# Routing stage of a decoder kernel: earlier gate loads, clearing on GpSimd, tables' arithmetic behind the counts, four context products ahead of them

## The reference, cut to what matters

```python
logits = x @ gate_w.T                      # 2048 tokens, 16 experts
expert, weight = argmax(logits), max(softmax(logits))
place = running count of earlier tokens with the same expert
keep  = place < 160                        # 160 = int(1.25 * 2048 / 16)
y[token] = weight * (relu(x @ w1[expert]) @ w2[expert]) if keep else 0
```

## Time and profile before

| | |
|---|---|
| median of 3 runs | 2365.23 us |
| lowest and highest | 2355.63 and 2367.0 us |
| the profiled execution, its own time | 2356.12 us |
| its span on the core | 2354.3 us |
| busy: PE, DVE, ACT, POOL | 2101.9, 1593.6, 1002.9, 886.1 us |
| the block `moe_route` in the trace | from 721.2 to 772.8 us |

### The profile page before, as it was taken

The page is one execution under the profiler, slowest core; times in us unless marked ns, Lnnn a source line. Parts: engine busy times, 40 slices in busy tenths (PEclk is TensorE's granted clock), DMA queues, the critical chain, the costliest instruction groups (busy, mean ns, idle before and its releaser), DMA issues. The chain is left out here.

```text
span 2354.3 us, 33922 instructions
## 1 busy us (share of the span) xinstructions
PE 2101.9 (89%) x12230; PEld 1455.0 (62%) x12230; DVE 1593.6 (68%) x4159; ACT 1002.9 (43%) x2133; POOL 886.1 (38%) x545
## 2 busy tenths in 40 slices
PE   8688888899996899698996888999898899999996
PEld 3255555554663799466483444448556788888886
DVE  6799999833657112556128996706687988888886
ACT  2498988623866231365425775241102221222110
POOL 0298888401642895333103665414211111110110
PEclk9799999999998999899997999999999999999998
DMA  3131111000005567300101000020300000000001
GB/s 103 47 94 50 50 50 47 17 12 1 1 1 194 188 227 231 117 2 2 61 1 43 1 1 23 21 81 1 143 1 3 1 1 1 1 1 1 1 1 37
DMA packets 63514, 109.35 MB, mean 46 GB/s; under 512 B 12530, under 2 KB 44146, under 8 KB 61620
## 3 DMA queue, kind: packets, MB, share of 16 engines
q1 hardware_dynamic: 61812, 102.99, 13.4%
q0 software_dynamic: 1536, 4.20, 0.5%
HBM read 94.19 MB, written 12.98 MB: 46 GB/s over the span
## 5 line engine op out<-in xcount | busy, mean ns | idle before, releaser
L781 POOL TENSOR_TENSOR XT<-mamba_DU,scan_BS 128x1024 f32<-128x1024 f32 x128 | 299.2, 2361 | 141.9 <-DMA scan_BS<-mamba_rows 104.2
L910 DVE TENSOR_TENSOR_SCAN scan_H<-scan_AB,XT 128x512 f32<-128x512 f32 x256 | 296.4, 1209 | 7.9 <-POOL XT L781 4.9
L3291 PE MATMUL ex_HP<-XT,pe_DOWN 128*128 128x256 f32 x1024 | 250.1, 391 | 6.0 <-PEq L3027 5.2
L3352 ACT ACTIVATE ex_GH<-ex_HP 128x512 f32<-128x512 f32 x128 | 76.5, 599 | 380.8 <-PE ex_HP L3291 346.1
L3322 PE MATMUL ex_OP<-pe_UP,ex_GH 128*128 128x256 f32 x1024 | 231.5, 380 | 0.0
L795 PEld LDWEIGHTS scan_TP<-ident,scan_H 128*128 128x128 f32 x1024 | 120.6, 142 | 156.8 <-DVE scan_H L910 79.8
L840 ACT ACTIVATE scan_AB<-mamba_E,mamba_AA 128x510 f32<-128x510 f32 x256 | 198.7, 776 | 37.2 <-DVE scan_H L910 32.9
L3291 PEld LDWEIGHTS ex_HP<-XT,pe_DOWN 128*128 128x128 f32 x1024 | 194.3, 194 | 31.8 <-issue 5.4
L3322 PEld LDWEIGHTS ex_OP<-pe_UP,ex_GH 128*128 128x128 f32 x1024 | 194.1, 190 | 26.2
L804 PE MATMUL scan_YT<-mamba_BC,ident 128*128 128x512 f32 x384 | 199.0, 601 | 4.1 <-ACT scan_YS L856 2.3
L3378 POOL TENSOR_TENSOR ex_AS<-ex_AS,pe_IV 128x512 f16<-128x512 f16 x32 | 52.9, 1682 | 363.4 <-DVE ex_AS L3426 363.4
(11 more groups left out here) (452 smaller groups left out, 4390.2 us busy)
## 6 DMA issues: line engine op xcount, KB each, us to landing
moe_W<-in_L_ffn_w SPq DMA_DIRECT2D x32, 1024.0 KB, 7.6
scan_BS<-mamba_rows SPq DMA_DIRECT2D x64, 256.0 KB, 3.2
pe_DOWN<-in_L_ffn_down SPq DMA_DIRECT2D x1, 4096.0 KB, 12.9
pe_UP<-in_L_ffn_up SPq DMA_DIRECT2D x1, 4096.0 KB, 22.3
moe_dispatch<-moe_BOTH SPq DMA_DIRECT2D x1, 2560.0 KB, 13.8
experts_XE<-moe_dispatch SPq DMA_DIRECT2D x16, 160.0 KB, 2.4
moe_answers<-experts_YE SPq DMA_DIRECT2D x16, 160.0 KB, 3.6
XT<-in_xT SPq DMA_DIRECT2D x4, 512.0 KB, 5.8
```

Of the source, the lines that this page charges most:

```text
L781: pool.tensor_tensor(BU[:, r % 2, cs], tokens(DU, cs, r // DS), row, ALU.mult).then_inc(bu_ready, 1)
L910: v.tensor_tensor_scan(H[:, r % 2, c], AB[:, n % 2, :], BU[:, r % 2, c], 0.0, ALU.mult, ALU.add).then_inc(h_ready, 1)
L3291: ins = pe.matmul(HP[:, n % 2, a, :], DOWN[:, k, 2 * q + a, :], XT[:, k, b * BLK:(b + 1) * BLK], start=(k == 0), stop=(k == KD - 1))
```

## The change

GW, EI and TI move from the routing block into the stage before: `MoeRest` is made in `xattn_inputs`, and SP issues their three loads at the start of the cross-attention's first block, behind two loads that were there. ZERO is set by POOL instead of DVE. DVE's `tables.exponents` moves from behind the copy to LS to behind the running sums; on ACT the step lengths stay in front, and Tanh and Sin move behind the softmax's exponentials. PE does the first four context products (all keys) ahead of the counts, instead of all twelve behind them.

```diff
@@ xattn_inputs
+    rest = MoeRest(nc, io)
     x = Inputs(nc, "xattn")
+    x.rest = rest
@@ stage_xattn
-            products(nc, "xproj", jobs, inputs.loads, ahead=[out_loads], joined=joined)
+            products(nc, "xproj", jobs, inputs.loads, ahead=[out_loads, inputs.rest.loads], joined=joined)
@@ ContextProducts
-    def tensor(self, pe):
+    def tensor(self, pe, first, last):
         self.loads.wait(pe)
-        for n in range(self.count):
+        for n in range(first, last):
@@ S4dTables
-    def steps_in_route(self, act):
+    def step_lengths(self, act):
         act.wait_ge(self.loaded, 32)
         act.activation(self.PAR[:, 0, :], self.PAR[:, 0, :], ACT.Exp).then_inc(self.dt_ready, 1)
+
+    def steps_in_route(self, act):
         act.wait_ge(self.exponents_ready, 1)
@@ MoeRest
+        self.GW = self.sb("GW", [P, KD, GPAD])
+        self.EI = self.sb("EI", [P, NE])
+        self.TI = self.sb("TI", [P, NT])
@@ moe_route, sync
-                sp.dma_start(GW[:], io["L0_ffn_gateT"].rearrange("(k p) n -> p k n", p=P)).then_inc(loaded, 16)
-                sp.dma_start(TRI[:], io["tri"]).then_inc(loaded, 16)
-                sp.dma_start(EI[:], io["expert_numbers"]).then_inc(loaded, 16)
-                sp.dma_start(TI[:], io["spill_rows"]).then_inc(loaded, 16)
+                sp.dma_start(TRI[:], io["tri"]).then_inc(tri_loaded, 16)
                 tables.load(sp)
                 context.loads.issue(sp)
                 sp.wait_ge(zero_ready, 1)
@@ moe_route, tensor
-                pe.wait_ge(loaded, 64)
+                rest.loads.wait(pe)
...
+                context.tensor(pe, 0, context.RING)
+                pe.wait_ge(tri_loaded, 16)
                 pe.wait_ge(onehot_ready, 1)
                 pe.matmul(CS[:].rearrange("p t e -> p (t e)"), TRI[:, 0, :], OH[:].rearrange("p t e -> p (t e)"), start=True, stop=False)
...
-                context.tensor(pe)
+                context.tensor(pe, context.RING, context.count)
@@ moe_route, scalar
-                tables.steps_in_route(act)
+                tables.step_lengths(act)
...
                 ins.then_inc(exp_ready, 1)
+                tables.steps_in_route(act)
@@ moe_route, vector
-                v.memset(ZERO, 0.0).then_inc(zero_ready, 1)
-                v.wait_ge(loaded, 64)
+                rest.loads.wait(v)
                 v.wait_ge(logits_ready, 1)
                 v.tensor_copy(LS[:], LT[:]).then_inc(logits_copied, 1)
-                tables.exponents(v)
...
                 v.sem_inc(onehot_ready, 1)
+                tables.exponents(v)
                 v.wait_ge(counted, 1)
@@ moe_route, gpsimd
+                pool.memset(ZERO, 0.0).then_inc(zero_ready, 1)
                 pool.wait_ge(routed, 1)
```

More of the change, by code:

```diff
@@ L1007, in stage_xattn @@
         finish_norm(nc, "xnorm", X, XT, ident, out_product, needs=[out_loads])
+    return inputs.rest
 def attention(nc, ident, QT, KT, V, X, BO, out_loads):
@@ L1362, with __init__ @@
 class MoeRest(Inputs):
-    def __init__(self, nc):
+    def __init__(self, nc, io):
         super().__init__(nc, "rest")
@@ L1369, in __init__ @@
         self.WT = self.sb("WT", [P, NT])
+        self.GW = self.sb("GW", [P, KD, GPAD])
+        self.EI = self.sb("EI", [P, NE])
+        self.TI = self.sb("TI", [P, NT])
+        self.pairs = [(self.GW[:], io["L0_ffn_gateT"].rearrange("(k p) n -> p k n", p=P)),
+                      (self.EI[:], io["expert_numbers"]), (self.TI[:], io["spill_rows"])]
+        self.ready()
         self.answers = nc.dram_tensor("moe_answers", (SLOTS, D), F32).ap()
@@ L1376, in stage_moe @@
     dispatch = nc.dram_tensor("moe_dispatch", (SLOTS + T, D), F32).ap()
-    rest = MoeRest(nc)
+    rest = inputs
     with Stage(nc, "moe") as st:
@@ L1384, in stage_moe, with moe_route @@
         tables = S4dTables(st, st, io)
-        context = moe_route(nc, io, X, XT, ident, TO, rest.FROM, rest.WT, dispatch, first_loads, tables)
+        context = moe_route(nc, io, X, XT, ident, TO, rest, dispatch, first_loads, tables)
         moe_experts(nc, io, ident, dispatch, rest.answers, rest.kernel, tables, context, W1, W2, first_loads)
     return rest
-def moe_route(nc, io, X, XT, ident, TO, FROM, WT, dispatch, first_loads, tables):
+def moe_route(nc, io, X, XT, ident, TO, rest, dispatch, first_loads, tables):
+    FROM, WT, GW, EI, TI = rest.FROM, rest.WT, rest.GW, rest.EI, rest.TI
     with Stage(nc, "route") as st:
-        GW = st.sb("GW", [P, KD, GPAD])
         LS = st.sb("LS", [P, G4])
         TRI = st.sb("TRI", [P, 2, P])
-        EI = st.sb("EI", [P, NE])
-        TI = st.sb("TI", [P, NT])
         ZERO = tables.BOTH[:].rearrange("p x d l -> p (x d l)")[:, 0:SLOTS // P * D]
@@ L1412, in moe_route @@
         CS = st.ps("CS", [P, NT, NE])
-        loaded = st.sem("loaded")
+        tri_loaded = st.sem("tri_loaded")
         zero_ready = st.sem("zero_ready")
```

## The result

The changed kernel takes 2381.0 us in the median of its 7 runs (2377.8 to 2391.61), against 2365.23 for the kernel before (7 runs, 2355.63 to 2381.61). The ratio is 1.0079, interval 1.0049 to 1.0109: slower, by 0.8%. The forecast was 2369.3, and the time lies outside its range. The lowest times differ by 22.2 us and the medians by 15.8; the runs of the kernel before spread by 26 us and those of the changed one by 14. The profiled execution took 2381.64, with a span of 2379.8 against 2354.3.

A forecast was written before the change was run, and what follows sets the result against it. PE was taken to bound the routing block: counts, then 30 us of context products. +2.8 us at the block's end and +1.3 for the table load gave +4.1 on 2365.23: 2369.3 us, range 2357 to 2374.

The forecast's parts named there:

- Parts 1 to 3: Routing block: earlier gate loads, POOL clearing (4.4 us), tables' arithmetic behind the sums; one-hot rows and sums 6.7 us earlier.
- Part 4, the order: PE's four key products ahead of counts wait for the last context load, landing at 734.9; counts reach DVE 4.8 us later.
- The rival of loads that are not late: Routing block: last context load lands at 728.9, block's end moves by -3.2 us, total 2363.3 us; chance 0.22.
- The sum that the forecast set beside it: Context loads: about 2.0 us plus bytes at 436 GB/s puts the 2.6 MB in place near 729.
- Part 4, the keys' length: PE's four key products start at 1.2 GHz, regain full clock after 5.0 us of work, and take 10.4 us.
- the 4.15 us that the forecast let pass: PE's wait from the counts' arrival until DVE's first copy ends and value product 1 starts.
- The same step for the values: PE's eight value products behind the counts: 0.315 us a record at full clock, 2.5 us each.
- it waits for the sixth copy: PE's value product 6 waits for DVE's sixth copy, starting 20.2 us behind the counts' arrival.
- The block's end: Routing block's end moves by the counts' delay minus 2.0 us: +2.8 us for counts 4.8 us late.
- The rival that came true: PE's clock stays at 1.2 GHz in the routing block: +13.8 us there, total 2380.3 us; chance 0.04.
- Part 5: Experts' block: a 1.28 us table load ahead of the first powers on ACT; PE waits 4.5 us instead of 3.2.
- Its term of +1.3: Uncovered table load in the experts' block adds 1.3 us to the total; 0 at the other bound.

The follow-up runs named there:

- keys_behind: Changed kernel with all twelve context products behind the counts again; 2354.68 us, ratio 0.9967.
- front_alone: Kernel before with only the four key products moved ahead of the counts, nothing else of the change; 2384.04 us, ratio 1.0077.
- burst: Changed kernel with eight extra, unread 128x512 products on PE behind the counts, none ahead of the keys; 2367.42 us, ratio 1.0007.
- warm: Changed kernel with ten extra, unread 128x512 products on PE between the logits' turning and the key products; 2376.83 us, ratio 1.0047.
- kick3: Changed kernel where PE waits for the context loads, then does three extra, unread products ahead of the keys; 2379.11 us, ratio 1.0063.
- warm_bridged: Changed kernel with ten extra, unread products on PE ahead of the keys and five behind the counts; 2374.61 us, ratio 1.0032.
- best: Changed kernel with context products behind the counts, seven extra products ahead of the counts, banks emptied 2, 3, 2, Exp table loaded early; 2350.12 us, ratio 0.9965.
- no_extra: Changed kernel with context products behind the counts, banks emptied 2, 3, 2, Exp table loaded early, no extra products; 2353.89 us, ratio 0.9953.
- primed: Changed kernel with one tiny Exp on ACT at the routing block's end, so the table loads there; 2381.4 us, ratio 1.0068.

## Why the prediction was wrong

**Parts 1 to 3 were right.** The gate products started at once; POOL's memset took 4.36 us (4.4 worked out) and held up nobody; the one-hot rows and sums were ready 12.0 us after the barrier, where 733.3 against 721.1 had meant 12.2.

**Part 4, the order, was right.** The keys waited for a context load, not for DVE. It landed at 736.11, 13.4 us after the barrier, against 13.8 forecast. The rival of loads that are not late did not come. The sum that the forecast set beside it, from the Trainium skill (DMA: Bandwidth & Descriptors, section Anatomy of one DMA), stands there for transfers on the gpsimd path, and SP issued these; by it the loads would have been in place some 8 us after the barrier, an estimate from that page, and not 13.4.

**Part 4, the keys' length, is the step that failed.** It read: "With 9 us of idling ahead, the products start at 1.2 GHz again. With 5.0 us of it: 5.7 records at 0.87, the other 10.3 at 0.53, together 10.4 us." The start at 1.2 GHz came true. The return did not: the keys took 16.10 us, and the counts behind them 2.1 instead of 1.6. That is +5.7 us on the keys, +0.5 on the counts. I had taken "5.0 us of work" from a stretch that began with the counts, and given it to a stretch that begins with keys. The experiments show the difference: counts first brought the clock back in before and in keys_behind, keys first did not in after, front_alone and burst.

The trace of the kernel before held one more return and a fall, which the forecast passed over:

```profile
727.00:728.00 1.00, 1.00 (x8) 0.00 (x0) 0.00 (x0) 0.42 (x1) 0.00 (x0) 0.56 1.10 287
731.00:732.00 1.00, 0.00 (x0) 0.00 (x0) 0.96 (x2) 0.87 (x1) 0.00 (x0) 0.64 0.87 165
```

The gate products brought the full clock 3.2 us behind their start at 724.66, and it was gone 1.6 us into the wait behind the turning. So the work ahead of a return ran from 3.2 to 7.1 us in one trace, and no one length of it could be carried over to other products; and the clock had been seen to fall in less idle time than the 4.15 us that the forecast let pass.

**The same step for the values** assumed 0.315 a record, the full clock, behind waits of 4.15 and 2 us. The wait came as forecast, 4.03. In the changed kernel the clock was low already; warm and kick3 show that this wait loses a clock that was full, and warm_bridged that 2.12 us do too. The forecast's "it waits for the sixth copy" did not show in the changed kernel, whose products of 4.6 us leave no gap in 36.98 us.

**The block's end** was to move by the delay of the counts minus 2.0 us. The counts reached DVE at 754.25 (31.5 us after the barrier), 10.5 us later than before (742.10, 21.0), so the rule gives +8.5; it moved by 21.8. The rule was worked out for values at the full clock, and here they had half of it. From the counts' arrival to the last copy's end it took 28.45 us in the forecast and took 795.95 - 754.25 = 41.7; the surplus of 13.2 is the second and larger part of the loss. 8.5 + 13.2 = 21.7.

**The rival that came true** had a chance of 0.04 and 2380.3 us: its mechanism is the one found, its time 0.7 us off the median. Its two prices were too low (keys 0.87, now 1.0 a record; value products 3.7, now 4.6), since neither came from a stretch of these products at the low clock. The four key records before had the returned clock in their last 0.4 us (0.53 in the window to 745), and the values' price came from count records. With its seven products at 4.6, its +13.8 would have been +20. That the median agrees so well is in part the luck of the medians: the lowest times are 22.2 us apart. "Against it: the clock came back after 5.0 and 7.1 us of work" was the only argument against it, and returns behind other work in one trace were thin ground for 0.04.

The Trainium skill (TensorE: Matmul & The Clock Gate, section "HAM oscillation — how this bites in real kernels") describes bursts of products between waits for a DMA, each burst starting at the low clock. The trace agrees for the start of the keys (8.36 us for route_WV, then 0.50), though here it is one wait with long work behind it. The trace does not agree with Part 1 of that page of the Trainium skill, by which everything issued behind a first stretch runs at the full clock: keys ran 16.10 us and values 36.98 at 0.50, without a gap.

**Part 5 was right in the load's place and in the wait**: a load of 1.28 us ahead of the powers, and PE waiting 4.58 us instead of 3.20, 4.5 forecast. Its term of +1.3 in the sum isn't borne out: the experts' block took 179.8 us against 180.1.

**What stays open.** Why counts ahead of the keys bring the clock back (1.9 us of them) and one extra product ahead of them (1.9 us as well) doesn't, each in the traces that there are. The trace shows one difference between the extra products and the keys. PEld's timeline of kick3, behind its first extra product:

```profile
739.77 0.34 PEld L1464 LDWEIGHTS route_WARM<-XT,ident 128*128 128x128 f32 x1 [0.52 <-issue]
740.62 0.34 PEld L1464 LDWEIGHTS route_WARM<-XT,ident 128*128 128x128 f32 x1 [0.52 <-issue]
```

Here a record comes every 740.62 - 739.77 = 0.85 us at the low clock; a key record of the same width takes 1.0. An estimate from the two is that the keys spend about 0.15 us a record on something other than the product itself, perhaps loads that nothing hides; PE's busy share of 1.00 doesn't show it. Every second key step also uses only 64 rows, and the matrices differ from `ident`. Which of these matters wasn't tried. Each kernel has one trace, and the return may have chance in it: the 35 runs of the kernel before beside burst reach from 2354.59 to 2389.01, with a mean clock of 0.960 at the lowest and 0.942 at the highest, which is more than the distance between the two kernels. keys_behind, best and no_extra too have one or two runs in twelve some 25 us above the others, at 0.946 to 0.950. No trace of such a run was taken, so whether they lose the clock in this block isn't shown. With the keys first and nothing ahead of them to hold the clock it is no chance: the 27 runs of after, front_alone and primed all took 2376.09 us or more, at 0.951 or less, while 27 of the 35 runs of before beside front_alone and primed took 2375.05 or less.

## What to carry to other kernels

Before you move work on PE across a wait, ask at which clock it will start and what brings the clock back; price both answers from rows at the low clock of the same kind of product, weight loads included. A wait of 2 to 4 us that looks cheap in the sum can cost four to seven times as much through the products behind it (16.9 us behind 4.03 in kick3, 14.6 behind 2.12 in warm_bridged), so it pays to reorder the copies that empty the banks. Put small urgent work (here the counts that DVE and POOL wait for) ahead of long work that waits for a load.

## What the runs showed of the hardware

- PE busy without a gap did not by itself bring the full clock: 36.98 us of 128x256 float products stayed at 0.50, while 2 us of 128x512 products with `ident` as weights, right behind 16 us of keys and the counts, brought it back (burst).
- The clock fell around waits of 4.03 us (warm, kick3), 2.12 us (warm_bridged), and in the product behind a wait of 1.44 us (keys_behind); it held behind 0.75 us (no_extra) and behind 1.17 and 1.30 (best). Each is one trace.
- A key step at the low clock costs 2.0 us against 1.05 (8.40 / 8), a value step 1.16 against 0.63 (20.05 / 32): 1.9 and 1.8 times.
- A float memset on POOL took 4.36 us for 5120 elements a partition, 0.85 ns each; the earlier trace rows had 0.86.
